# A thin chain of products laid out anew between the steps of an attention loop, on one core

## The reference

```
x = x + o(attention(rms(q(ln(x))), rms(k_img), v_img) over the first 257 context tokens
        + attention(rms(q(ln(x))), rms(k), v)         over the other 767)        # 16 heads of 32
y = ln(x)
thought = layer_norm(y)[:, -1, :] @ agg_w + agg_b        # one row of each batch
for _ in range(4):
    t = gelu(layer_norm(thought) @ d1_w + d1_b)          # 512 -> 2048
    thought = thought + t @ d2_w + d2_b                  # 2048 -> 512
z = y + sigmoid(y @ gate_w + gate_b) * (thought @ bc_w + bc_b)
x = x + layer_norm(z)
```

## Time and profile before

| | |
|---|---|
| median of three runs | 599.85 us |
| the profiled execution | 598.93 us |
| its span, first to last instruction | 597.1 us |
| PE busy | 531.0 us (89%) |
| DVE / ACT / POOL busy | 378.5 / 304.8 / 238.5 us |
| mean granted TensorE clock | 0.952 |

### The profile page before, as it was taken

One profiled execution on the slowest core, in us unless ns is written; L12 is line 12 of the kernel. 1 busy time (PEld: TensorE's weight loads), 2 busy tenths in 40 slices (PEclk: granted clock), 3 DMA queues, 4 the chain that ended last, 5 costly groups with the idle time before them and its releaser, 6 DMA issues.

```text
span 597.1 us, 9907 instructions
## 1 busy us (share of the span) xinstructions
PE 531.0 (89%) x3800; PEld 325.1 (54%) x3800; DVE 378.5 (63%) x767; ACT 304.8 (51%) x536; POOL 238.5 (40%) x138
## 2 busy tenths in 40 slices
PE   2597889999999999999999987899999989999860
PEld 2476768987655655555555554444454544554330
DVE  5447967433977677557775776566555756348766
ACT  2355754543146667446765443646463464585441
POOL 0034230032034776437655342161533345477353
PEclk9789999999979999999999977999999999799976
DMA  8506668599499678946897472707072713100001
GB/s 287 190 2 230 234 241 316 186 211 329 166 211 328 180 191 200 242 121 133 233 231 201 127 172 72 171 1 172 9 164 72 173 36 111 71 1 37 18 35 53
DMA packets 56511, 91.92 MB, mean 154 GB/s; under 512 B 5552, under 2 KB 30256, under 8 KB 55952
## 3 DMA queue, kind: packets, MB, share of 16 engines
q1 hardware_dynamic: 52000, 75.26, 46.0%
q0 software_dynamic: 3184, 14.16, 7.1%
q10 hardware_dynamic: 1280, 1.88, 1.1%
HBM read 71.08 MB, written 19.40 MB: 152 GB/s over the span
## 4 chain that ended last, share of the span: by engine, by line
PE 71%; DVE 15%; ACT 7%; issue 3%; POOL 2%; DMA 2%; POOLq 0%; ACTq 0%; SPq 0%; DVEq 0%
PE psum L766 12%; PE psum L672 12%; PE psum L747 11%; PE psum L729 11%; PE psum L771 6%; PE psum L803 5%; PE psum L892 4%; DVE negt L1168 3%; PE psum L838 2%; PE psum L857 2%; PE psum L792 1%; PE psum L665 1%; DVE fst L1109 1%; DVE negt L1166 1%; POOL ssum L1341 1%
## 5 line engine op out<-in xcount | busy, mean ns | idle before, releaser
L1000 ACT ACTIVATE prob<-psum 128x512 f32<-128x512 f32 x256 | 138.8, 594 | 131.0 <-PE psum L747 130.3
L1168 DVE TENSOR_REDUCE negt<-psum 128x1 f32<-128x255 f32 (+1 forms) x256 | 129.2, 546 | 0.0
L1391 POOL TENSOR_TENSOR added<-added,prob 128x1024 f32<-128x1024 f32 x48 | 113.6, 2366 | 19.7 <-ACT prob L1000 15.2
L729 PE MATMUL psum<-kst,qst 96*128 96x512 f32 x256 | 99.2, 464 | 3.7 <-DVE negt L1168 3.6
L1388 POOL TENSOR_TENSOR added<-prob 128x1024 f32<-128x1024 f32 x16 | 37.9, 2369 | 157.7 <-ACT prob L1000 157.7
L1166 DVE TENSOR_REDUCE negt<-psum 128x1 f32<-128x257 f32 x128 | 53.5, 418 | 70.7 <-PE psum L729 70.1
L747 PE MATMUL psum<-qst,kst 112*128 112x256 f32 x512 | 94.5, 304 | 1.8 <-ACT prob L1000 1.8
L747 PEld LDWEIGHTS psum<-qst,kst 112*128 112x128 f32 x512 | 80.7, 197 | 25.5 <-ACT prob L1000 11.2
L766 PE MATMUL psum<-prob,vring 128*32 128x256 f32 x1152 | 92.8, 406 | 0.0
L729 PEld LDWEIGHTS psum<-kst,qst 96*128 96x128 f32 x256 | 40.8, 193 | 63.1 <-issue 40.9
L1341 POOL TENSOR_TENSOR ssum<-sq 128x512 f32<-128x512 f32 x6 | 9.8, 1633 | 108.3 <-ACT sq L965 108.3
(11 more groups left out here) (153 smaller groups left out, 673.8 us busy)
## 6 DMA issues: line engine op xcount, KB each, us to landing
kst<-kscr SPq DMA_DIRECT2D x96, 256.0 KB, 5.8
vring<-vscr SPq DMA_DIRECT2D x16, 576.0 KB, 7.9
kscr<-hl SPq DMA_DIRECT2D x16, 512.0 KB, 3.0
d<-d POOLq DMA_DIRECT2D x8, 1024.0 KB, 6.6
qst<-qscr SPq DMA_DIRECT2D x96, 64.0 KB, 6.0
vscr<-vbuf SPq DMA_DIRECT2D x18, 256.0 KB, 3.2
raw<-ctxT SPq DMA_DIRECT2D x4, 1024.0 KB, 6.3
qscr<-hl SPq DMA_DIRECT2D x8, 512.0 KB, 4.5
```

Of the source, the lines that this page charges most:

```text
L729: pe.matmul(psum[:, n % 3, :], qst[0:96, slot, jj, qt * P:(qt + 1) * P], kst[0:96, slot, jj, half * 512:(half + 1) * 512], start=True, sto ...
L1000: act.activation(prob[:, r % NP, part], score2[:, part], ACT.Exp).then_inc(exp2_done, 1)
L1168: dve.tensor_reduce(negt[:, u % 2, qt, half, HPG + j:HPG + j + 1], psum[:, n % 3, k0:512], AX.X, ALU.max, negate=True)\
L1391: pool.tensor_tensor(added[:, :], added[:, :], prob[:, r % NP, :], ALU.add).then_inc(added_done, 1)
```

## The change

The chain's events get other steps. No event of the chain stands in positions 4 and 5 any more, but for the gelu, which needs no PE, and `o(2, 0)`. Each `ch_d1` and each `ch_d2` stands whole in one step. Between `ch_gelu` and `ch_hT` and in some other places there are more steps. The output products stand at steps given in a table, and those of k = 2 move from 98 and 99 to 100 and 104. Where a sum falls on step 104, it stands behind S1 (`behind`). The statistics of `o` go to a buffer of their own.

```diff
-CHUNKS = 2
+O_AT = ((34, 35), (66, 67), (100, 104), (8 * NU + 2, 8 * NU + 2))
...
-    def closed(s):
+    def behind(step, *e):
+        post.setdefault(step, []).append(e)
+        if e[0] == 'ch_stat':
+            post[step].append(('ch_rstd', e[1]))
 
-        while any((s + n + ahead) % 8 == 1 for n in range(1, KC // CHUNKS)):
+    def free(s):
+
+        while s % 8 in (4, 5):
             s += 1
         return s
...
-    at(s + 5, 'ch_turn', 0)
-    at(s + 6, 'ch_agg')
-    at(s + 6, 'ch_stat', 2)
-    s += 7
+    s = free(s + 6)
+    at(s, 'ch_turn', 0)
+    s = free(s + 1)
+    at(s, 'ch_agg')
     for k in range(K_STEPS):
-        at(s, 'ch_ln', 2 + k)
-        at(s + 1, 'ch_turn', 1 + k)
-        s = closed(s + 2)
+        (behind if s in O_AT[2] else at)(s, 'ch_stat', 2 + k)
+        at(s + 1, 'ch_ln', 2 + k)
+        s = free(s + 2)
+        at(s, 'ch_turn', 1 + k)
+        s = free(s + 1)
         for kc in range(KC):
-            at(s + kc // CHUNKS, 'ch_d1', k, kc)
-        s += KC // CHUNKS
-        at(s, 'ch_gelu', k)
-        at(s + 1, 'ch_hT', k)
-        s = closed(s + 2)
+            at(s, 'ch_d1', k, kc)
+        at(s + 1, 'ch_gelu', k)
+        s = free(s + 3)
+        at(s, 'ch_hT', k)
+        s = free(s + 1)
         for m in range(KC):
-            at(s + m // CHUNKS, 'ch_d2', k, m)
-        s += KC // CHUNKS
-        at(s, 'ch_sum', k)
-        if k < K_STEPS - 1:
-            at(s, 'ch_stat', 3 + k)
-        s += 1
+            at(s, 'ch_d2', k, m)
+        s = free(s + 1)
+        (behind if s in O_AT[2] else at)(s, 'ch_sum', k)
+    s = free(s + 2)
     at(s, 'ch_turn', 1 + K_STEPS)
     at(s + 1, 'ch_bc')
-    at(s + 2, 'ch_spread', 0)
-    at(s + 2, 'ch_spread', 1)
-    s += 3
+    s = free(s + 3)
+    at(s, 'ch_spread', 0)
+    at(s, 'ch_spread', 1)
     at(s, 'res2')
...
     for k in range(4):
-        s = 8 * NG * (k + 1) + 2
         for n in range(2):
-            while s in cut:
-                s += 1
-            extra.setdefault(s, []).insert(n if k == 3 else 0, ('o', k, n))
-            s += 1 if k < 3 else 0
+            extra.setdefault(O_AT[k][n], []).insert(n if k == 3 else 0, ('o', k, n))
...
-                stats(residual(f), fst[:, f % 2, :], mv[:, f, :]).then_inc(x2_stats, 1)
+                stats(residual(f), bst[:, f, :], mv[:, f, :]).then_inc(x2_stats, 1)
```

More of the change, by code:

```diff
@@ L226, in make_plan @@
         s += F_EVERY if s < 8 * NU else F_TAIL
-    cut = {s for s, es in extra.items() for e in es if e[0] in ('ch_d1', 'ch_d2', 'f_gate') and e[2] > 0
-           and not any(x[:2] == e[:2] and x[2] == 0 for x in es)}
     for k in range(4):
-        s = 8 * NG * (k + 1) + 2
         for n in range(2):
-            while s in cut:
-                s += 1
-            extra.setdefault(s, []).insert(n if k == 3 else 0, ('o', k, n))
-            s += 1 if k < 3 else 0
+            extra.setdefault(O_AT[k][n], []).insert(n if k == 3 else 0, ('o', k, n))
     for t in range(10, ahead):
```

## The result

The changed kernel takes 614.59 us, the median of four runs (612.71 to 618.38), and the kernel before 599.62 us beside it (four runs, 598.74 to 602.08). The ratio is 1.025, interval 1.019 to 1.031. On another chip it was 615.47 against 601.89 us, 1.021 (1.014 to 1.027). It is 15 us slower, where I had said 602 and at most 608.

What follows compares the result with a forecast made beforehand. PE was taken as the bound up to step 127, so only its waits and half-clock time could differ. Terms summed to -5.4, plus 7.8 for clock falls, +2.4 on 598.93 us; adjusted to the median, 602, range 595.5 to 608.

Steps and rivals of the forecast that it cites:

- I take three falls: +7.8: Clock term, steps 72 to 126: three falls to half clock at 2.6 us each, added to -5.4 without falls.
- six places: Steps 74, 83, 90, 98, 105 and the spreads at 118, where PE waits might bring the clock down.
- a sign of being wrong: Forecast wrong if position 1 norms take 0.5 us, half-clock pieces number under two or over four, or end grows under 4.
- Start of the chain, -9.1: Steps 72 to 79: loss falls from 11.9 to 2.8 us; the stall in step 74 stays, between S1 matmuls.
- Gelu, -1.8: Gelus at 82, 92, 100 and 108: waits total 5.6 us against 7.4; S2 still waits for the next exponentials.
- Sums at position 0, +6.6: Sums, norms and turns at positions 0, 1, 2: 8.5 us lost against 1.9, from late exponentials and POOL clashes.
- no clash at position 1: Rival, chance 0.10: DVE reaches the norms at 89 and 97 before POOL starts; 595.6 us.
- Steps 112 to 126, -6.7: Output products and the stretch 112 to 126: 38.2 us against 44.9, half-clock time taken out.
- The end, +5.6: Behind step 127: one more tile's turn and gate follow the output products, between 5.3 and 7.7 us.
- slower: Rival, chance 0.18: waits bring five to six clock falls, 607.5 to 611, said as 608 us.

Runs made afterwards that it cites:

- run with work in the waits: Changed kernel plus two unused 128x128 by 512-column matmuls ahead of S1 or the turn in steps 74, 83, 90, 98 and 105: 601.89 us, 0.999 to the kernel before.
- the joined one: Kernel before with only steps 72 to 88 rearranged, using the changed kernel's start and an earlier second norm: 590.61 us, 0.981; repeated 588.08 us, 0.976.
- run with the end alone: Kernel before up to step 112, then the changed kernel's places (turn 5 at 114, ch_bc 115, spreads and tiles from 118): 605.35 us, 1.006.

## Why the prediction was wrong

The step that failed is "I take three falls: +7.8", and with it the range. The first profile has seven pieces where I had counted six places and taken three. They cost about 15.0 us: over steps 72 to 111 the stretches lose 30.2 us beyond bare steps and products (17.44 us a unit and 42.5 us, as in the prediction), the waits and other losses at full clock come to 16.8 of it (the first three points below), and 13.4 remain for the clock; 1.6 us are its piece in step 119 and 120 (32.8 us in 116 to 126, 31.2 in the run with the product at 101, where none fell there). The second profile bears the size out: over steps 72 to 111 it had 10.2 us more at half and took 4.2 us longer, 0.41 for each, which makes 14.0 of the 34.1 us here. The price per piece was near (2.6 taken, 2.1 measured), the count was not, and more than four pieces was a sign of being wrong that the prediction itself had named. I had one wait of 1.92 us without a fall against three with, and took the odds at a half. In the changed kernel the five waits of 1.72 to 1.92 us all brought one, in both profiles, and so did the wait of 1.3 us in step 109, which I had not counted because before it brought none. The run with work in the waits shows that this is the cause, not a companion: the same clashes, nearly no falls, 12.7 us.

Over all 13 profiles there are 40 waits of PE of 1.7 us or more between steps 72 and 127. The clock fell during 33 of them or at most 2.4 us behind them. Six of the seven others are one place, the turn behind the gelu in step 109 (1.92 or 1.93 us in the kernel before, the joined one and their variants), the seventh is step 105 in the run without table loads. So the one wait without a fall from which I took even odds was a matter of its place, and what sets that place apart was not tested. Of the waits of 1.3 us in steps 93 and 109 nine of 12 brought a fall, of those of 1.4 us in step 116 none of seven.

Point by point:

- *Start of the chain, -9.1.* Right in its mechanism: the wait of step 74 stayed, between the two S1 matmuls, 1.87 us. `ch_ln` 2 and the steps to 80 ran free. At full clock the lost time is about 3.1 us, where 2.8 had been worked out (in the run with work in the waits the clock stayed up here, step 74 was as long as in the changed kernel, and the eight steps took 21.6 us). But the longest piece at half clock (13.66 us) lies there.
- *Gelu, -1.8.* 5.6 us forecast for four places; 2.1, 1.8, 0.5 and 1.8 measured against the same steps of the bare unit, 6.2. Right.
- *Sums at position 0, +6.6.* 8.5 forecast: steps 88 to 90 lost 2.3, 96 to 98 2.5, 104 to 106 2.7, together 7.5. Right, and here the rival "no clash at position 1" fell with the norm at 1.90 us. That step 105's norm would run free because it starts ahead of POOL's addition was my estimate, which no row of before shows; it was ahead by 0.49 us and ran in 0.53.
- *Steps 112 to 126, -6.7.* -2.8, and -4.4 without the piece at half clock. 112 to 115 was right (9.34 for 9.4). 116 to 126 was 2.4 us too low: steps 118 and 121 took 5.3 and 3.4 us where I had 4.6 and 2.8.
- *The end, +5.6.* +6.5; the run with the end alone gives +6.3.
- *The 2.9 us ahead of step 72* were no part of any term. They belong to this execution: in the profile of the kernel before the same part was among the shortest, so that the sum started from a low base.

Sum of the misses on the profiled span: 7.2 of the clock, 2.9 ahead of step 72, 2.3 in 112 to 126, 0.9 at the end, -0.1 in the waits: 13.2, against 612.5 - 599.5 = 13.0. What of the rivals came true was "slower": it has the right mechanism and up to six falls, 608 where 614.6 was measured. Whether the remaining difference between the two profiles' pieces follows a rule is open; no run was made to settle it.

## What to carry to other kernels

A wait of PE costs twice where the clock falls behind it, here 1.7 to 1.9 us for the wait and some 2.1 for the piece at half clock. In this kernel a wait of 1.7 us or more brought a fall in 33 of 40 cases, and in nearly all the rest it was the same place that did not, so count the falls place by place and as likely, not as even; a wait of 1.3 us can bring one too (nine of 12). Before a dependent step is moved a few places, look at what each engine does in the new place (here POOL's additions at positions 1 to 4, the table loads, ACT's three instructions at position 0), for the same norm took 0.53 us or 1.9 to 2.9 by its place. And when a gap cannot be closed, unused matmuls in it can be cheaper than the gap (12.7 us in the changed kernel, nothing in the joined one), as long as the clock would fall there and the matmuls do not wait for the same thing.

## What the runs showed of the hardware that I had not expected

- The clock stayed at half for 13.66 us with PE busy in all of it (first window above), in steps 75 to 78, which hold hardly more than attention; the four pieces of 3.4 us behind steps 90, 98, 105 and 109 lay on a whole `ch_d1` or `ch_d2`. The second profile of the same kernel has 13.7 us there again, and 10.2 behind step 83; but a piece that reached into a step with a whole product was 6.8 us there (step 107) and in the run with the product at 101 (step 91), so no run settles what ends a piece. That PE is busy does not bring the clock back at once: here it was busy for 13.66 us at a granted clock of 0.50.
- A DVE instruction that starts ahead of POOL's addition can still lose. In the kernel with the first norm moved, the norm began at 357.32, 0.22 us ahead of the addition, and took 2.88 us, to 0.28 us behind the addition's end. POOL was issuing a DMA from 356.75 to 357.52. In step 105, with no DMA, 0.49 us of lead was enough. The kernel before has another case that lost, which the prediction put down as caught by POOL like the first, the norm of step 76, 0.01 us ahead of the addition and with no DMA beside it:

```profile
361.42 2.64 DVE L1226 TENSOR_SCALAR chx<-th,cmv,crs 32x512 f32<-32x512 f32 x1
361.43 2.35 POOL L1391 TENSOR_TENSOR added<-added,prob 128x1024 f32<-128x1024 f32 x1 [2.62 <-ACT prob L1000]
```

  In the 13 profiles the norm lost with leads of 0.01 (two cases, 2.64 us) and 0.22 us (2.88 us), and ran in 0.53 with 0.42 to 0.49 us (nine cases) and with 0.93 us (four cases). So a norm that was ahead by 0.42 us and more ran free each time, and at the small leads the start that the profile records did not decide. What does decide there, and what in the two engines holds the norm, no run shows. Whether the DMA's issue played a part in the case of 0.22 us is open; the two of 0.01 us had none.
- The two profiles of the changed kernel have the same waits and not the same pieces (37.5 and 47.8 us at half, one behind step 93 only in the second), but the falls behind the five waits of 1.72 to 1.92 us were in both, and the wait of 1.92 or 1.93 us in step 109 of the kernel before, the joined one and their variants brought none in six profiles.
